# A recommender tower on one core: whole grams with sixteen gathers behind each, one-hot rows of two tables at a time, and another order in chunk 0 and in the last MLP

## The reference

```python
e = jnp.stack([tbl_0[ids[:, 0]], tbl_1[ids[:, 1]], ..., tbl_25[ids[:, 25]]], axis=1)
combined = jnp.concatenate([e, r_dense_x[:, None, :]], axis=1)
z = jnp.einsum('bfd,bgd->bfg', combined, combined)[:, _TRIU_I, _TRIU_J]
h = jnp.concatenate([z.reshape(z.shape[0], -1), r_dense_x], axis=1)
h = jnp.maximum(h @ W_top1 + b_top1, 0.0)
h = jnp.maximum(h @ W_top2 + b_top2, 0.0)
y = h @ W_top3
```

## Time and profile before

| | us |
|---|---|
| median of 3 runs | 373.29 |
| lowest and highest | 373.04, 374.13 |
| profiled execution | 374.87 |
| span of its profile | 373.1 |

### The profile page before, as it was taken

How to read it: one execution, slowest core, us unless ns; L and a number is a source line. 1 busy time by engine, 2 the same in 40 slices (tenths; PEclk the granted TensorE clock), 3 DMA queues, 4 the chain that set the end, 5 groups by cost and what they waited for, 6 DMA issues and landing times.

```text
span 373.1 us, 13958 instructions
## 1 busy us (share of the span) xinstructions
PE 339.7 (91%) x6176; PEld 312.7 (84%) x6176; DVE 194.0 (52%) x700; ACT 184.3 (49%) x234; POOL 254.9 (68%) x265
## 2 busy tenths in 40 slices
PE   0775879599999999999999999999999999999986
PEld 0775879598989988999989989999888988998776
DVE  1998758274645734575645634575545635541020
ACT  3783711673337463573437552582526552574332
POOL 6877777777777777777777777776777677771000
PEclk9998999999999999999999999999999999999999
DMA  7974761221532216222432126221442122210000
GB/s 266 368 244 157 223 215 53 52 66 53 177 87 67 57 52 208 57 66 52 145 115 72 51 54 206 51 72 47 121 142 67 46 59 66 53 50 26 16 2 4
DMA packets 15777, 37.17 MB, mean 100 GB/s; under 512 B 5125, under 2 KB 7813, under 8 KB 15716
## 3 DMA queue, kind: packets, MB, share of 16 engines
q0 software_dynamic: 8192, 16.79, 16.8%
q1 hardware_dynamic: 7524, 19.48, 15.5%
HBM read 36.24 MB, written 0.01 MB: 97 GB/s over the span
## 4 chain that ended last, share of the span: by engine, by line
PE 86%; POOL 5%; issue 4%; ACT 3%; DMA 3%; ACTq 0%
PE ps_lk L442 38%; PE ps_gram L469 14%; PE ps_tr L454 8%; PE ps_mlp L499 8%; PE ps_zt L499 7%; POOL rows L218 5%; PE ps_mlp L508 4%; PE ps_zt L508 4%; DMA rows<-in_tbl,gather_ids 2%; PE ps_mlp L516 2%; PE ps_zt L486 2%; ACT xt L319 1%; ACT xt L309 1%; DMA gather_ids<-in_ids_gather 1%; ACT ids_from L304 0%
## 5 line engine op out<-in xcount | busy, mean ns | idle before, releaser
L218 POOL DMA_INDIRECT rows<-in_tbl,gather_ids x256 | 253.5, 990 | 82.3 <-issue 70.7
L252 DVE TENSOR_SCALAR onehot<-ids_from 128x256 fp32r<-128x256 f32 x640 | 151.7, 303 | 59.3 <-PE ps_lk L442 42.6
L442 PE MATMUL ps_lk<-onehot,table 128*128 128x256 f32 x1280 | 166.9, 289 | 13.2 <-DVE onehot L252 11.5
L442 PEld LDWEIGHTS ps_lk<-onehot,table 128*128 128x128 f32 x1280 | 159.1, 195 | 13.9 <-issue 12.4
L319 ACT COPY xt<-ps_tr 128x512 f32<-128x512 f32 x64 | 76.6, 1197 | 96.5 <-PE ps_tr L454 94.6
L260 DVE STREAM_TRANSPOSE zs<-ps_gram 128x832 f32<-128x832 f32 x16 | 16.8, 1050 | 91.9 <-PE ps_gram L469 91.9
L469 PEld LDWEIGHTS ps_gram<-xt 128*26 128x26 f32 x4096 | 43.5, 103 | 19.5 <-issue 16.0
L469 PE MATMUL ps_gram<-xt 128*26 128x26 f32 x4096 | 52.2, 192 | 5.5 <-issue 1.3
L309 ACT COPY xt<-ps_lk 128x512 f32<-128x512 f32 x40 | 48.6, 1226 | 13.4 <-PE ps_lk L442 7.9
L454 PE MATMUL ps_tr<-ident,rows 128*128 128x128 f32 x256 | 39.9, 278 | 9.2 <-ACT xt L319 4.5
L454 PEld LDWEIGHTS ps_tr<-ident,rows 128*128 128x128 f32 x256 | 29.8, 141 | 13.2 <-issue 5.3
(11 more groups left out here) (30 smaller groups left out, 102.4 us busy)
## 6 DMA issues: line engine op xcount, KB each, us to landing
ids<-in_ids_onehot SPq DMA_DIRECT2D x16, 640.0 KB, 5.2
rows<-in_tbl,gather_ids POOLq DMA_INDIRECT x256
w<-in_tbl SPq DMA_DIRECT2D x6, 512.0 KB, 5.8
h<-in_tbl SPq DMA_DIRECT2D x2, 512.0 KB, 5.9
zt<-in_tbl SPq DMA_DIRECT2D x2, 512.0 KB, 5.7
dense_x<-in_dense SPq DMA_DIRECT2D x8, 128.0 KB
zt<-in_dense SPq DMA_DIRECT2D x8, 128.0 KB, 2.4
w<-in_w SPq DMA_DIRECT2D x1, 512.0 KB
```

What stands on the lines that cost most here:

```text
L218: pool.indirect_dma_start(rows[n % ROW_BUFS][:, r, :], None, t_[f"tbl_{GATHERED[r]}"], bass.IndirectOffsetOnAxis(ap=gather_ids[:, n, r:r + ...
L252: nc.vector.tensor_scalar(onehot[:, u % RING, :], ids_from[:, j, :], float(k), None, ALU.is_equal).then_inc(s_unit, 1)
L442: m = nc.tensor.matmul(bank(c, i)[:, j % 2, :], table[:, j, part, k, :], onehot[:, u % RING, :], start=(k == 0 and part == 0), stop=(k == ...
```

## The change

1. *Gathers.* All sixteen gathers of tile n wait for both parts of gram n−2. The wait on `s_tr` and the increment of a carrier semaphore are gone. The first tiles are no longer issued freely: the second to fifth batch of eight gathers wait for counts of `s_unit_used` (`LEAD`), and the sixth for gram(0, 0).
2. *Grams.* The two parts of a gram stand next to each other in TensorE's list. `gram(c, 0)` now comes after layer1(c−1, 2), `gram(c, 1)` after layer2(c−1, 1) and turn(c+1, 0, 2).
3. *One-hot rows.* One VectorE instruction makes the rows of block k for two tables, 512 elements. A unit is now such a pair, the ring holds 8 of them (one lookup, as before), `s_unit_used` counts two of them as one step (8 matmuls; before it was 4), and a lookup waits twice instead of eight times (in chunk 0 before each unit). The ids are loaded and shifted in parts of 4 and 6 tables instead of 5 and 5.
4. *Chunk 0.* Lookups and turns of chunk 0 alternate one by one; the turns of tile (1, 0) stand in chunk 1's part of the list instead of before it.
5. *Last MLP.* Both tiles of the last chunk go through layer 1, then both through layer 2, then layer 3 (`last1`, `last2`, `last3`), in the banks of the lookups, `ps_tr`, `ps_mlp` and `ps_zt`. The layer 2 of the chunk before is done before the last gram.

```diff
+RING = 8
+UNITS = LP * KT
+USE = 2
...
+CUT = (0, 4, NO)
...
+LEAD = (0, 2, 6, 10, 16)
...
             def gather(n, g):
-                if n >= ROW_BUFS:
-                    pool.wait_ge(s_tr, (n - ROW_BUFS) * NGR + g + 1)
-                    pool.sem_inc(s_carrier["pool"], 1)
                 for r in GROUPS[g]:
...
-            for n in range(ROW_BUFS):
-                for g in range(NGR):
-                    gather(n, g)
-
-            for n in range(ROW_BUFS, TILES):
+            for n in range(TILES):
                 for h in range(2):
-                    pool.wait_ge(s_gpart, (n - 2) * PARTS + h + 1)
+                    b = n * PARTS + h
+                    if 0 < b < len(LEAD):
+                        pool.wait_ge(s_unit_used, LEAD[b])
+                    elif b >= len(LEAD):
+
+                        if n < ROW_BUFS or h == 0:
+                            pool.wait_ge(s_gpart, (max(n - 2, 0) + 1) * PARTS)
                     gather(n, 2 * h)
                     gather(n, 2 * h + 1)
...
-                    nc.vector.tensor_scalar(onehot[:, u % RING, :], ids_from[:, j, :],
+                    nc.vector.tensor_scalar(onehot[:, u % RING, :, :], ids_from[:, 2 * i:2 * i + 2, :],
                                             float(k), None, ALU.is_equal).then_inc(s_unit, 1)
...
-                for j in (2 * i, 2 * i + 1):
+                if c == 0:
+                    pe.wait_ge(s_low, 2 * i + 2)
+                for k in range(KT):
+                    u = i * KT + k
                     if c == 0:
-                        pe.wait_ge(s_low, j + 1)
-                    for k in range(KT):
-                        u = j * KT + k
-                        if k % 2 == 0:
-                            pe.wait_ge(s_unit, c * UNITS + u + 2)
+                        pe.wait_ge(s_unit, u + 1)
+                    elif k % (KT // 2) == 0:
+                        pe.wait_ge(s_unit, c * UNITS + u + KT // 2)
+                    for j in range(2):
                         for part in range(2):
...
             for c in range(1, CHUNKS):
                 turn_pairs(c - 1, 0)
...
+                else:
+                    turn(c, 0, 3)
                     layer3(c - 2)
                 lookup(c, 3)
                 turn_pairs(c - 1, 1)
...
                 layer1(c - 1, 0)
-                gram(c, 0, 0)
...
                 layer1(c - 1, 2)
+                gram(c, 0, 0)
                 gram(c, 0, 1)
                 turn(c, 1, 2)
                 layer1(c - 1, 3)
...
                 layer2(c - 1, 0)
-                gram(c, 1, 0)
                 if c + 1 < CHUNKS:
                     turn(c + 1, 0, 0)
                     lookup(c + 1, 2)
                     turn(c + 1, 0, 1)
-                    layer2(c - 1, 1)
+                layer2(c - 1, 1)
+                if c + 1 < CHUNKS:
                     turn(c + 1, 0, 2)
-                    gram(c, 1, 1)
+                gram(c, 1, 0)
+                gram(c, 1, 1)
```

More of the change, by code:

```diff
@@ L371, in _ @@
             evac_group(0, 1, 3)
-            act.wait_ge(s_gpart, PARTS)
-            for g in range(NGR - 1):
-                evac_group(1, 0, g)
             act.wait_ge(s_cols, 16)
@@ L477, in turn_pairs @@
                     pe.wait_ge(s_zt, c * CT + t)
[L478 to L482 removed]
+                elif c > 0:
                     pe.wait_ge(s_act, (c - 1) * MLP_USES + T1 + T2)
```

261 lines of the change are left out of this document (142 added, 119 removed).

## The result

| | before | changed |
|---|---|---|
| median us | 373.71 (4 runs beside it) | 411.88 (409.71 to 419.94, 4 runs) |
| ratio | 1 | 1.099 (95%: 1.094 to 1.104) |
| span of the profile | 373.1 | 407.8 |
| mean granted clock of TensorE | 0.995 | 0.958 |

The changed kernel is 38 us slower. The forecast was 374.5 us with a range up to 380.5: slower was the likeliest sign, the size is wrong by 37 us. Some executions on the same chip are a few per cent slower at a lower granted clock (one of the four here, 419.94, and two of the four each of late_gates_third and halves_apart_again, the profiled one of the latter among them); the ratios leave them out, and without them the medians are 410.1, 401.3 and 400.2 us.

The account below looks back on a forecast made before the run. TensorE bound the kernel, with GpSimd's gathers only 1.3 us per chunk behind. Later gathers make loops 43.95 us instead of 42.35; with chunk 0 and a 15.9 us tail the span is 374.3, median 374.5 us, range 369.5 to 380.5.

Parts of the forecast that it names:

- its loop: Steady part, end of gram(c, 0) to end of gram(c+1, 0): 0.6 + 20.2 + 1.4 + 19.4 + 2.35 = 43.95 us against 42.35.
- Part 2: Gathers waiting for whole gram n−2: first eight lose about 10 us of lead, 1.6 us per chunk is lost.
- first leg: End of gram(c, 0) until group 3 lands for turn(c+1, 0, 3): wake, sixteen gathers and landing, 22.2 us.
- the wake: GpSimd's start of the next gather after the gram it waits for, taken as 0.6 us.
- the landing: From the end of a tile's last gather until its rows are in, with semaphore, taken as 1.4 us.
- Part 1: Joining gram halves saves about 0.1 us per gram; a whole gram takes 2.25 us without gathers, 3.3 with them.
- The waits before turn(c+1, 0, 2) and turn(c+1, 0, 3): TensorE waits each chunk for gathered rows: 2.3 us before the first turn, another 1 us before the second.
- Part 3: One-hot instructions of 512 elements in the lookups: hidden behind TensorE, put at nothing.
- port rule: GpSimd's DMA issue needs a port pair VectorE holds in two-port modes; longer one-hot instructions would slow gathers.
- Part 4: Chunk 0: GpSimd's stream moves back 1.0 us, but the new order wins 2.6 us; gram(2, 0) ends at 133.2.
- Part 5: Loops and last MLP: four loops, last gram ending at 358.4, then a tail of 15.9 us instead of 18.9.
- the loop stretches: Rival in the gather loop: slower gathers (6.7 us), a clock drop or instructions running out; 377 to 384 us, chance 0.20.

Follow-up runs that it names:

- late_gates_third: The kernel before with one edit: all sixteen gathers of a tile wait for both parts of gram n−2; 401.3 us, ratio 1.071.
- halves_apart_again: The changed kernel with the two parts of grams apart again, other work between them, gathers still waiting for whole grams; 400.2 us, ratio 1.070.

## Why the prediction was wrong, step by step

The legs of its loop, forecast and measured in the changed kernel in six chunks:

| leg | forecast | measured |
|---|---|---|
| end of gram(c, 0) to turn(c+1, 0, 3) | 22.2 | 25.95, 23.13, 22.92, 21.22, 22.98, 25.41 |
| from there to gram(c+1, 0) | 19.4, last 15.5 | 19.32, 19.32, 19.81, 20.14, 21.04, 19.34 |
| the gram | 2.35 | 2.71, 2.62, 4.59, 5.12, 5.10, 2.47 |

The last five of the six, from the end of gram(2, 0) on, are 235.2 us against 215.9: 19.3 of the 33.5 us by which the span is too long. 9.6 lie before the end of gram(2, 0) (142.77, forecast 133.2), 3.3 between the ends of gram(7, 0) and gram(7, 1), 1.3 in the tail (17.2, forecast 15.9).

Two steps failed, and about equally: the sum had 9.6 us for the late gates, which cost 27 alone, and a gain for the whole gram, which costs 22 alone.

- *Where the gathers start (Part 2).* The mechanism and the sum of its first leg were right where the late gates act without holes: 22.25 to 22.8 in halves_apart_again. In the changed kernel itself the leg is not set by the gathers, since turn(c+1, 0, 3) waits in no chunk; its length is TensorE's own work, holes and half clock, and a value near 22.2 there is chance. In halves_apart_again the wake within it was 0.36, not 0.6, and the landing 1.6 to 2.1 (212.04 to 213.68, 208.41 to 210.51 in halves_apart_again and late_gates_third), not 1.4; the errors cancel.
- *What a wait costs.* The first step that failed. The sum took a wait of 2.3 us at its own length. Measured, a wait of 1.7 to 2.65 us was followed by 3.4 or 6.8 us at half clock in nine of ten chunks (late_gates_third and halves_apart_again), up to 3.4 us more. The prediction had the row, the lookup of 5.15 us in the earlier trace rows, and named the clock as part of a rival, but priced neither the turn and layer beside that lookup nor the six repetitions. Late gates alone make the chunk 47.0 us long where it was 42.3: 4.7 us a loop in place of 1.6. In the profile, four such loops (18.8), 2.4 us before them and 6.5 in the last loop are 27.7 of the 28.2 us by which its span is longer.
- *Grams in one piece (Part 1).* The second step that failed. The whole gram of 2.25 or 3.3 us was wrong: 2.5 to 2.7 without a hole before the next piece of work, 4.6 to 5.1 with one (the table above). The sums are off as well: two halves of 1.20 less 0.1 are 2.3, and 1.55 + 1.75 less 0.1 are 3.2. "A gram of 128 matmuls in one piece may run out of instructions, which no row shows" stood as a clause in a rival and had no price. A row did show it. The idle time "issue" of the gram, 16.0 us in the earlier trace rows, was read as gather stalls throughout, but the table of waits of the kernel before has one among the 63 that is five times as long as a gather's 0.2 to 0.28 us:

```profile
PEld ps_gram L469 <- issue: 16.0, 63, 1.4
```

  It is the hole at 52.66 of the table above. Sorting the gaps by length and looking at the instruction packets beside the longest would have led to the mechanism.
- *The waits before turn(c+1, 0, 2) and turn(c+1, 0, 3).* In the changed kernel the second is missing, the first is there in three chunks with 0.8 to 1.3 us in place of 2.3, and in the three others turn(c+1, 0, 0) waits, 1.3 to 2.8 us. In that of 153.49 the four gathers began by 146.88, and 3 packets of their queue start between 147.0 and 150.0 while the ids of the next chunk come in, 768 KB in one load:

```profile
153.49 0.63 PE L476 MATMUL ps_tr<-ident,rows 128*128 128x128 f32 x4 [2.16 <-DMA rows<-in_tbl,gather_ids]
```

```profile
149.00:152.00 3.00, 2.32 (x13) 1.76 (x12) 1.20 (x4) 0.48 (x1) 2.39 (x3) 1.00 0.95 353
```

  (The last two numbers are the DMA's busy share and GB/s.) The sum had no term for this load, which stood in slack before. That it is the cause is argued from the trace; no run moved the load.
- *One-hot rows (Part 3).* Right for the time, 42.28 us a chunk with them. But the gathers do feel them: in the changed kernel a gather during which VectorE makes one-hot rows takes 1.046 us in the mean (65 of 122 over 1.05 us), and one during which VectorE does nothing 0.947 (1 of 95); before, with 256 elements, it was 1.000 (6 of 128) and 0.948. All seven kernels with 512 elements on chips of the 373 us kind have 1.04 to 1.05 us, all four with 256 have 0.99 to 1.00. That is the direction of the port rule that the prediction took from the Trainium skill, page "SBUF — State Buffer", section "SBUF: two separate sides"; in which mode the instructions ran no row shows. Over all gathers it is 18 ns, 0.3 us per tile, where the rival had 0.07 us per gather.
- *Chunk 0 (Part 4).* The first batch was held until 16.69 (forecast 15.5 and the wake, 16.1), but TensorE's new order puts a half-clock lookup ahead of gram(0, 0). The 2.6 us to be won did not come. In the changed kernel gram(1, 0) ends at 94.79, before 94.72, with three holes of 3.5 us in sum ahead of it; the 9.6 us of gram(2, 0) come behind that, with the wait at 106.00 (2.83 us, 6.8 us at half clock) and the hole at 117.15. What the new chunk 0 brings or costs by itself stays open.
- *The last MLP (Part 5).* Right: 15.6 us without disturbance, forecast 15.9.
- *The rivals.* The true case was the first, "the loop stretches", with 0.20 and 377 to 384 us: by the clock and the instructions that run out, and by 16 × 0.018 × 6 = 1.7 us of the 6.7 of its slower gathers. It priced one mechanism at a time, and that of the instructions not at all. The range stopped at 380.5 because of these prices.

## What to carry to other kernels

A loop that is short of slack by 2 us can lose more than 2 us a round: if TensorE is what waits, it loses the wait and often the clock behind it, and moving one small operation behind other work can save most of it (20 of 26 us here). Very short instructions must not stand in long runs: here 512 in 2.15 us needed two portions of 256 that came no faster than one per 3.45 us once nothing was in store, and work of 2.2 us or more between the halves took nearly all holes away. Sort "issue" gaps by length before naming their cause.
